# Results scattered without add and summed per batch, in a static order of blocks

## The chip, the cores and the metric

One core of a Trainium2 chip runs one layer of a small language model. The metric is the device time of one execution in microseconds (us); less is better.

## The reference

Each of 8 x 512 tokens looks up 36 angles, a circuit of six qubits turns them into six expectation values, and these are projected to an embedding of 192. An attention layer and a mixture of experts with two of eight experts per token follow, each behind a layer norm and added to its input.

```python
def reference(x, L0_tok_quantum_params, ...):
    h = _L0_tok_ref(x, L0_tok_quantum_params, L0_tok_post_w, L0_tok_post_b)
    h = h + _L0_attn_ref(_layernorm(h, axis=-1), L0_attn_W_qkv, L0_attn_b_qkv)
    h = h + _L0_ffn_ref(_layernorm(h, axis=-1), L0_ffn_Wg, L0_ffn_W1, L0_ffn_b1, L0_ffn_W2, L0_ffn_b2)
    return h

def _L0_ffn_ref(x, Wg, W1, b1, W2, b2):
    gate_scores = jnp.einsum('bsd,de->bse', x, Wg)
    topk_scores, topk_idx = jax.lax.top_k(gate_scores, K)          # K = 2, E = 8
    topk_probs = jax.nn.softmax(topk_scores, axis=-1)
    h = jax.nn.gelu(jnp.einsum('bsd,edh->bseh', x, W1) + b1, approximate=False)
    y = jnp.einsum('bseh,eho->bseo', h, W2) + b2
    y_sel = jnp.take_along_axis(y, topk_idx[..., None], axis=2)
    return jnp.sum(topk_probs[..., None] * y_sel, axis=2)
```

## The kernel before

The kernel is written out by hand, engine by engine; each engine runs its own list in order, and semaphores hold the lists together. It has three parts.

The *front* (to about 190 us) computes the circuit and, batch by batch, attention, the gate scores and the residual. In its last iterations VectorE finds the two experts of each token of a batch (`route_and_root`), the row at which the token goes into that expert's region (`slots`), and its share (`shares`). GpSimd scatters the tokens' 32 features into `routed`, a scratch tensor in device memory with a region of rows for each expert: `scatter(b, k)`, eight scatters of 128 rows for each batch, 64 in all. TensorE computes the residual of the batch (`residual`), ScalarE copies it to `hres` (`h2_copy`), and SyncE stores it to `out` (`store`).

The *table*: when all batches are routed, `counts` sums the tokens of each expert, and VectorE works out (`block_table`) for each of 71 blocks of 128 rows which expert it has (`t_exp`) and at which row of `routed` it starts (`t_i`). Blocks stand in the order of experts; there are 64 + 7 of them so that every split of the tokens fits, and the last ones can be empty. A second table says up to which block all additions must have landed before a block may be scattered, since a token's two results are added to the same row of `out`.

The *blocks*: four blocks make a step. SyncE loads a block's rows into `xb` (`load_block`, 16 blocks ahead); TensorE transposes a step (`block_transpose`), picks the step's four up projections (`pick_up`, from VectorE's `expert_of`) and applies them (`up_proj`); ScalarE applies gelu; TensorE multiplies with the expert's down projection (`down_proj`) into one of two buffers; VectorE weights the result into one of eight buffers `y` (`weighted`); GpSimd adds it to `out` by an indirect scatter with add. SyncE counts the scatters that have landed in `landed`:

```python
for m in range(BLOCKS):
    last_shared = pool.value_load(t_i[0:1, 1, m:m + 1], min_val=1, max_val=BLOCKS + 1)
    pool.wait_ge(y_done, m + 1)
    pool.wait_ge(landed, last_shared)
```

## Time and profile before

| | us |
|---|---|
| median of 3 runs (lowest, highest) | 389.87 (388.54, 391.79) |
| span of the profiled execution | 338.6 |
| median less that span | 51.3 |
| GpSimd busy in the span | 250.2 (74%) |
| TensorE matmul busy | 240.9 (71%) |
| VectorE busy | 177.6 (52%) |
| ScalarE busy | 95.2 (28%) |

The span runs from the first to the last instruction that the profiler records on the core; what the timed runs have beside it (loading, start and end) isn't in the profile. The profiled execution has no time of its own beside its span, so it is set beside the median of the runs. GpSimd's busy time on a scatter is the time of the instruction, and the transfer lands later.

### The profile page before, as it was taken

What the parts mean: (1) busy time and instruction counts of PE and PEld (TensorE: products, weight loads), DVE (VectorE), ACT (ScalarE), POOL (GpSimd) and SP (SyncE); (2) the same over time, 40 slices, a digit from 0 to 9 for tenths busy, and PEclk for the clock granted to TensorE, in tenths of its full rate; (3) what the DMA queues carried; (4) which work ended last, traced back from release to release, by engine and by line L of the source; (5) the groups of instructions that cost most, each with busy time, mean ns of one, the idle gap of its engine ahead of it and who ended that gap; (6) DMA issues with size and microseconds to landing.
All of it is one profiled execution on the core that took longest, in us unless ns stands there. A gap on an engine that the chain in (4) does not pass through costs nothing. (4 is left out here: it accounts for less than half of the span.)

```text
span 338.6 us, 6221 instructions
## 1 busy us (share of the span) xinstructions
PE 240.9 (71%) x1585; PEld 162.0 (48%) x1585; DVE 177.6 (52%) x698; ACT 95.2 (28%) x223; POOL 250.2 (74%) x283
## 2 busy tenths in 40 slices
PE   0831973668478989768654899999999587999500
PEld 0621641223243445444421678777777365877400
DVE  5758997488998866684699322232222122122200
ACT  1002001354324144634233323332432132133000
POOL 5778979309968777766777388888883888888673
PEclk9999995558955556965555599999999799699955
DMA  6710019900000001111123146656461556564510
GB/s 191 201 13 11 0 45 400 382 5 2 2 0 9 12 13 60 63 57 60 59 70 103 22 54 69 64 62 67 53 69 18 60 62 65 61 69 50 59 10 0
DMA packets 28141, 22.61 MB, mean 67 GB/s; under 512 B 15434, under 2 KB 25546, under 8 KB 27787
## 3 DMA queue, kind: packets, MB, share of 16 engines
q0 software_dynamic: 13296, 7.95, 21.1%
q1 hardware_dynamic: 14524, 14.23, 13.0%
q8 instruction: 15, 0.25, 0.3%
q14 instruction: 18, 0.15, 0.2%
q10 hardware_dynamic: 288, 0.03, 0.1%
HBM read 7.25 MB, written 15.63 MB: 68 GB/s over the span
## 5 line engine op out<-in xcount | busy, mean ns | idle before, releaser
L709 POOL DMA_INDIRECT out<-up x71 | 110.3, 1554 | 33.1 <-issue 13.9
L1972 PE MATMUL bank_b<-down,up 128*128 x426 | 91.2, 354 | 5.0 <-DVE up L1473 1.0
L1972 PEld LDWEIGHTS bank_b<-down,up 128*128 128x128 f32 x426 | 72.9, 200 | 22.6 <-issue 18.8
L1473 DVE TENSOR_SCALAR up<-bank_b,up 128x192 f32<-128x192 f32 x71 | 29.6, 418 | 97.5 <-PE bank_b L1972 84.9
L657 POOL DMA_INDIRECT routed<-rows,slot x64 | 61.9, 968 | 23.9 <-issue 18.0
L472 POOL DMA_INDIRECT theta_all<-angles,ids x32 | 32.4, 1012 | 10.9 <-issue 9.0
L1651 ACT ACTIVATE up<-bank_a 128x384 f32<-128x384 f32 x71 | 31.3, 497 | 3.4 <-PE bank_a L1962 2.9
L1775 PE MATMUL bank_b<-queries_t,keys_t 32*128 32x512 f32 x64 | 26.1, 900 | 6.9 <-ACT keys_t L1499 3.4
L1782 PE MATMUL bank_a<-keys_t,wt 32*128 32x512 f32 x64 | 27.6, 949 | 3.8 <-DVE nmax L1133 2.1
L1663 ACT COPY up<-bank_c 128x384 f32<-128x384 f32 x18 | 8.6, 478 | 61.8 <-PE bank_c L1951 58.7
L1133 DVE TENSOR_REDUCE nmax<-bank_a 128x2 f32<-128x1024 f32 x16 | 19.5, 1219 | 11.5 <-PE bank_a L1782 11.3
L1521 ACT ACTIVATE prob<-bank_b 128x1024 f32<-128x1024 f32 x16 | 16.4, 1023 | 18.2 <-PE bank_b L1775 18.2
L1951 PE MATMUL bank_c<-up_all,up 128*128 128x384 f32 x36 | 16.6, 545 | 6.6 <-DVE up L1418 4.4
L1962 PE MATMUL bank_a<-up 32*128 32x128 f32 x426 | 18.5, 304 | 0.6 <-ACT up L1657 0.5
L1962 PEld LDWEIGHTS bank_a<-up 32*128 32x128 f32 x426 | 15.1, 201 | 5.6 <-issue 4.5
L1848 PE MATMUL bank_a<-m,a2t 32*128 32x192 f32 x64 | 14.3, 536 | 4.8 <-ACT hres L1529 2.7
L1848 PEld LDWEIGHTS bank_a<-m,a2t 32*128 32x128 f32 x64 | 7.7, 277 | 11.9 <-issue 10.6
L1794 PE MATMUL bank_c<-prob,u 128*32 128x128 f32 x256 | 12.6, 361 | 0.8 <-ACT prob L1521 0.7
L1657 ACT COPY up<-bank_d 128x128 f32<-128x128 f32 x18 | 4.8, 266 | 25.3 <-PE bank_d L1944 25.3
L1775 PEld LDWEIGHTS bank_b<-queries_t,keys_t 32*128 32x128 f32 x64 | 7.1, 255 | 9.9 <-issue 8.6
L1794 PEld LDWEIGHTS bank_c<-prob,u 128*32 128x32 f32 x256 | 9.3, 145 | 5.0 <-ACT prob L1521 2.3
L1951 PEld LDWEIGHTS bank_c<-up_all,up 128*128 128x128 f32 x36 | 6.9, 212 | 8.5 <-issue 3.3
(420 smaller groups left out, 369.4 us busy)
## 6 DMA issues: line engine op xcount, KB each, us to landing
routed<-pad_rows SPq DMA_DIRECT2D x8, 528.0 KB, 5.7
out<-hres SPq DMA_DIRECT2D x8, 384.0 KB, 2.4
down<-down_w SPq DMA_DIRECT2D x1, 2304.0 KB, 11.9
up<-up_w SPq DMA_DIRECT2D x1, 1536.0 KB
out<-up POOLq DMA_INDIRECT x71, 3.5
up<-routed SPq DMA_DIRECT2D x69, 16.0 KB
routed<-rows,slot POOLq DMA_INDIRECT x64
up<-up_w SPq DMA_DIRECT2D x1, 780.0 KB
```

Source lines behind the costliest of these rows:

```text
L472: pool.indirect_dma_start(out=theta_all[:, t, :], out_offset=None, in_=angles, in_offset=bass.IndirectOffsetOnAxis(ids[:, b, j:j + 1], 0)) ...
L657: pool.indirect_dma_start(out=routed, out_offset=bass.IndirectOffsetOnAxis(slot[:, b, k, j:j + 1], 0), in_=rows[:, b, k, j, :], in_offset=None
L709: pool.indirect_dma_start(out=out_rows, out_offset=bass.IndirectOffsetOnAxis(xb[:, m // STEP % RING, m % STEP, DEST:DEST + 1].bitcast(I32) ...
L1473: dve.tensor_scalar(y[:, m % RESULTS, :], bank_b[:, m % 2, 0:D], xb[:, m // STEP % RING, m % STEP, SHARE:SHARE + 1], None, ALU.mult).then_ ...
L1651: act.activation(hid[:, n, :], bank_a[:, n, 0:HID], ACT.Gelu).then_inc(gelu_done, 1)
L1775: mm = pe.matmul(bank_b[:, n, :], keys_t[r, bt % 3, k * P:(k + 1) * P], queries_t[r, :], start=True, stop=True)
L1782: mm = pe.matmul(bank_a[:, n, :], wt[r, bs % 2, :], keys_t[r, bs % 3, :], start=True, stop=True)
L1794: mm = pe.matmul(bank_c[j * F:(j + 1) * F, 0:P], u[:, b * TILES + k, :], prob[:, k, j * P:(j + 1) * P], start=(k == 0), stop=(k == TILES - 1),
L1848: mm = pe.matmul(bank_a[:, 2 + n, 0:D], a2t[r, :], m2[r, :], start=True, stop=True)
L1951: pe.matmul(bank_c[:, 0:HID], pick[:, s % 2].rearrange("p n f -> p (n f)"), up_all[:, :], start=True, stop=True).then_inc(picked, 1)
L1962: mm = pe.matmul(bank_a[:, n, c * P:(c + 1) * P], up_now[r, s % 2, c * P:(c + 1) * P], xt[r, 0, :], start=True, stop=True)
L1972: mm = pe.matmul(bank_b[:, m % 2, 0:D], hid[:, m % STEP, c * P:(c + 1) * P], down[:, bass.ds(first + c * D, D)], start=(c == 0), stop=(c = ...
```

## The change

Results are no longer added to `out` where they land. Each token has a row for its first and one for its second expert in a new scratch tensor `results` (2 x 4096 rows of 192), and GpSimd scatters each block there without add and without a wait on other scatters. The residual stays in `hres`. SyncE loads the results of one batch at a time back into `prob` and `keys_t`, VectorE adds both to `hres` (`add_results`), and SyncE stores the batch.

So that a batch is whole before the last block, the order of the blocks is now by groups: the full blocks that the first four batches give (at least 25, so 25 of them stand in an early table that is made while batches 4 to 7 are still in the front), then what batches 3, 4, 5, 6 and 7 complete, one group each. After block `whole_after(b)` batch b has all its results. A late table with the other 46 blocks is made after the front; TensorE spreads it over the partitions (`late_columns`). The first 16 blocks are loaded as soon as the early scatters have landed, and the first two picks and the first transposition stand inside the front's loop.

The batches are summed after fixed blocks (`SUM_AT`), loaded and stored after fixed blocks (`STORE_AT`, `whole_after`); the last batch is loaded when the last block with tokens has landed, and summed and stored in two halves.

```diff
+    EARLY = 2 * EARLY_BATCHES * SEQ // P - (E - 1)
+    LATE = BLOCKS - EARLY
+    LEAST = 2 * TOKENS // P
+    results = nc.dram_tensor("results", (2 * TOKENS, D), F32, kind="Internal").ap()
+    results_view = results.rearrange("(k b p j) d -> b p k (j d)", k=2, b=BATCHES, j=TILES)
...
+        def whole_after(b):
+
+            return 2 * SEQ * (max(b + 1, EARLY_BATCHES)) // P + E - 2
...
+        SUM_AT = (46, 48, 53, 55, 59, 62)
+        STORE_AT = (45, 47, 51, 53, 57, 60)
...
+            def load_results(b):
+                sp.dma_start(results_in[b % 2], results_view[b]).then_inc(results_back[b % 2], 16)
+
+            def store(b):
+                sp.wait_ge(summed, b + 1)
+                sp.dma_start(out_view[b], hres[:, b, :]).then_inc(out_done, 16)
+
             sp.wait_ge(table_done, 1)
...
+            sp.wait_ge(scattered_early, 16 * 2 * TILES * EARLY_BATCHES)
+            for m in range(RING * STEP):
+                load_block(m)
+            for m in range(LEAST - 1):
                 sp.wait_ge(added[m % RESULTS], 16 * (m // RESULTS) + 16)
...
+                following = m + RING * STEP
+                if following == EARLY_STEPS * STEP:
+                    sp.wait_ge(table_done, 2)
+                    sp.wait_ge(scattered_late, 16 * 2 * TILES * (BATCHES - EARLY_BATCHES))
+                if following < BLOCKS:
+                    load_block(following)
+                if m == whole_after(0):
+                    load_results(0)
+                    load_results(1)
+                for b in range(BATCHES - 2):
+                    if m == STORE_AT[b]:
+                        store(b)
+                        if b < 3:
+                            load_results(b + 2)
+                for b in (5, 6):
+                    if m == whole_after(b):
+                        load_results(b)
+            last = sp.value_load(need[0:1, 0:1], min_val=1, max_val=BLOCKS - LEAST + 1)
+            sp.wait_ge(landed, last)
...
+            sp.wait_ge(summed, BATCHES - 2)
+            for h, cut in enumerate(LAST_HALVES):
+                sp.dma_start(results_in[1][:, :, cut], results_view[BATCHES - 1][:, :, cut]).then_inc(half_back[h], 16)
+            store(BATCHES - 2)
+            for h, cut in enumerate(LAST_HALVES):
+                sp.wait_ge(summed, BATCHES + h)
+                sp.dma_start(out_view[BATCHES - 1][:, cut], hres[:, BATCHES - 1, cut]).then_inc(out_done, 16)
...
-            pool.wait_ge(h2_out, 16 * BATCHES)
-            pool.wait_ge(order_done, 1)
             for m in range(BLOCKS):
-                last_shared = pool.value_load(t_i[0:1, 1, m:m + 1], min_val=1, max_val=BLOCKS + 1)
                 pool.wait_ge(y_done, m + 1)
-                pool.wait_ge(landed, last_shared)
-                hold(pool)
                 pool.indirect_dma_start(
-                    out=out_rows, out_offset=bass.IndirectOffsetOnAxis(
+                    out=results, out_offset=bass.IndirectOffsetOnAxis(
                         xb[:, m // STEP % RING, m % STEP, DEST:DEST + 1].bitcast(I32), 0),
-                    in_=y[:, m % RESULTS, :], in_offset=None, bounds_check=TOKENS - 1,
-                    oob_is_err=False, compute_op=ALU.add).then_inc(added[m % RESULTS], 16)
+                    in_=y[:, m % RESULTS, :], in_offset=None, bounds_check=2 * TOKENS - 1,
+                    oob_is_err=False).then_inc(added[m % RESULTS], 16)
...
+            early_table()
+            expert_of(0)
+            expert_of(1)
+
             for i in range(LAST[0] + 2, BATCHES + 2):
                 variance2(i - 2)
...
-            block_table()
-            expert_of(0)
-            expert_of(1)
...
+            late_table()
+            late_numbers()
+
+            def add_results(b, k):
...
+                if k == 0:
+                    dve.wait_ge(results_back[b % 2], 16 * (b // 2) + 16)
+                else:
+                    join()
+                last = dve.tensor_tensor(hres[:, b, :], hres[:, b, :], results_in[b % 2][:, k, :], ALU.add)
...
+                for b in range(BATCHES - 2):
+                    if m in (SUM_AT[b], SUM_AT[b] + 1):
+                        add_results(b, m - SUM_AT[b])
+            add_results(BATCHES - 2, 0)
+            add_results(BATCHES - 2, 1)
+            for h, cut in enumerate(LAST_HALVES):
+                part = hres[:, BATCHES - 1, cut]
+                dve.wait_ge(half_back[h], 16)
+                step(dve.tensor_tensor(part, part, results_in[1][:, 0, cut], ALU.add))
+                join()
+                dve.tensor_tensor(part, part, results_in[1][:, 1, cut], ALU.add).then_inc(summed, 1)
...
+            act.activation(gelu_ahead[:, :], half_pi[:, 0:1], ACT.Gelu)
             a2t_copy(BATCHES - 1)
             h2_copy(BATCHES - 1, 0)
             h2_copy(BATCHES - 1, 1)
-            act.activation(gelu_ahead[:, :], half_pi[:, 0:1], ACT.Gelu)
...
+            for m in range(LEAST - 1, BLOCKS):
+                act.wait_ge(added[m % RESULTS], 16 * (m // RESULTS) + 16)
+                act.sem_inc(landed, 1)
...
+                if i == BATCHES:
+                    pick_up(0)
+                    pick_up(1)
+                    block_transpose(0)
 
             residual(BATCHES - 1, 0)
             residual(BATCHES - 1, 1)
-            pe.wait_ge(table_done, 1)
-            pick_up(0)
-            pick_up(1)
             pe.wait_ge(down_in, 16)
             pe.wait_ge(h2_copied, 2 * BATCHES)
-            block_transpose(0)
             up_proj(0)
+            late_columns()
             for m in range(BLOCKS):
```

VectorE, ahead of the front's last four iterations; `nmax` is the row maximum of batch 7, `t` the copy with which batch 4 is routed. Before:

```order
L1133 TENSOR_REDUCE nmax<-bank_a 128x2 [waits s_done]
L1178 COPY t<-bank_a 128x96 [waits t2_done]
L1181 TENSOR_TENSOR var_p<-t,ev 128x64 [waits t2_copied]
L1184 TENSOR_REDUCE var_s<-var_p 128x4 [waits dve_step]
L1186 TENSOR_SCALAR ve<-var_s 128x4 [waits dve_step]
```

And now (`angle_stages` holds the table's work space, `up` the picks):

```order
L1167 TENSOR_REDUCE nmax<-bank_a 128x2 [waits s_done]
L1418 TENSOR_SCALAR full_i<-full_i 128x8
...
L1425 TENSOR_TENSOR angle_stages<-blk,cum 128x175 [waits dve_step]
L1428 TENSOR_REDUCE t_exp<-angle_stages 128x25 [waits dve_step]
L1429 TENSOR_TENSOR angle_stages<-angle_stages,skip 128x175
L1432 TENSOR_REDUCE t_skip<-angle_stages 128x25 [waits dve_step]
L1433 TENSOR_SCALAR up<-t_exp,own 128x25
L1434 TENSOR_SCALAR t_i<-t_exp 128x25
L1436 SCALAR_TENSOR_TENSOR t_i<-blk,t_skip 128x25 [waits dve_step]
L1495 TENSOR_TENSOR up<-feature,up 128x128 x2
L1214 COPY t<-bank_a 128x96 [waits t2_done]
```

The early table and two picks, 19 instructions, stand between the row maximum and the routing of batch 4.

TensorE, where the front's iteration for batch 5's residual (`bank_a<-m,a2t`) begins. Before:

```order
L1813 MATMUL bank_a<-var_w,at 128x96 [waits at_copied]
L1838 MATMUL bank_a<-ident,ev 128x128 [waits h2_copied,wt_copied,gates_done]
L1848 MATMUL bank_a<-m,a2t 128x192 [waits wt_copied,h2_copied,t2_copied,a2t_copied]
L1848 MATMUL bank_a<-m,a2t 128x192
L1848 MATMUL bank_a<-m,a2t 128x192 [waits wt_copied,h2_copied,t2_copied,a2t_copied]
```

And now:

```order
L1887 MATMUL bank_a<-var_w,at 128x96 [waits at_copied]
L1918 MATMUL bank_a<-ident,ev 128x128 [waits h2_copied,wt_copied,gates_done]
L1946 MATMUL bank_b<-up_all,up 128x384 [waits exp_done,pick_done] x2
L1935 MATMUL bank_d<-ident,up 128x128 [waits block_in0]
L1928 MATMUL bank_a<-m,a2t 128x192 [waits wt_copied,h2_copied,t2_copied,a2t_copied]
```

The two picks and the first transposition of a block step moved here from behind the last residual.

VectorE at the end of the program, `up<-bank_b` being the weighting of a block. Before nothing stands behind the last one; now:

```order
L1538 TENSOR_SCALAR up<-bank_b,up 128x192 [waits added6,y_mm]
L1528 TENSOR_TENSOR hres<-hres,prob 128x768 [waits results_back0]
L1528 TENSOR_TENSOR hres<-hres,prob 128x768 [waits dve_step]
L1553 TENSOR_TENSOR hres<-hres,keys_t 128x384 [waits half_back0]
L1555 TENSOR_TENSOR hres<-hres,keys_t 128x384 [waits dve_step]
L1553 TENSOR_TENSOR hres<-hres,keys_t 128x384 [waits half_back1]
L1555 TENSOR_TENSOR hres<-hres,keys_t 128x384 [waits dve_step]
```

Batch 6 is added whole and batch 7 in halves, after the weighting of all 71 blocks.

## Rows read from the trace of the kernel before

**Rows 1.** The page's granted clock, in tenths of full speed, 40 slices of 8.5 us

```profile
PEclk9999995558955556965555599999999799699955
```

**Rows 2.** Groups by line: count, busy us and mean ns, idle before and its releasers

```profile
L709 POOL DMA_INDIRECT out<-up x71 | 110.3, 1554 | 33.1 <-issue 13.9 <-SPq L446 9.7 <-DVE up L1473 9.4
...
L657 POOL DMA_INDIRECT routed<-rows,slot x64 | 61.9, 968 | 23.9 <-issue 18.0 <-DVE ev L1162 5.6 <-DVE slot L1269 0.3
```

**Rows 3.** Timeline of GpSimd: start us, us, instruction, idle before and releaser

```profile
189.19 0.96 POOL L657 DMA_INDIRECT routed<-rows,slot  x1 [0.31 <-issue]
...
252.54 1.55 POOL L709 DMA_INDIRECT out<-up  x1 [0.30 <-issue]
256.87 1.55 POOL L709 DMA_INDIRECT out<-up  x1 [2.77 <-issue]
...
322.71 1.55 POOL L709 DMA_INDIRECT out<-up  x1 [2.83 <-issue]
...
332.01 1.56 POOL L709 DMA_INDIRECT out<-up  x1 [0.30 <-issue]
```

**Rows 4.** Timeline of VectorE in the block stage: blocks 5, 37, 41, 65 and 70

```profile
201.56 0.42 DVE L1473 TENSOR_SCALAR up<-bank_b,up 128x192 f32<-128x192 f32 x1 [0.84 <-PE bank_b L1972]
...
253.77 0.42 DVE L1473 TENSOR_SCALAR up<-bank_b,up 128x192 f32<-128x192 f32 x1 [0.98 <-PE bank_b L1972]
...
264.36 0.42 DVE L1473 TENSOR_SCALAR up<-bank_b,up 128x192 f32<-128x192 f32 x1 [4.13 <-DMA out<-up]
...
311.13 0.42 DVE L1473 TENSOR_SCALAR up<-bank_b,up 128x192 f32<-128x192 f32 x1 [0.87 <-PE bank_b L1972]
...
318.26 0.42 DVE L1473 TENSOR_SCALAR up<-bank_b,up 128x192 f32<-128x192 f32 x1 [0.72 <-PE bank_b L1972]
```

**Rows 5.** Timeline of VectorE, GpSimd and TensorE where batch 4 is routed

```profile
140.93 0.25 DVE L1178 COPY t<-bank_a 128x96 f32<-128x96 f32 x1
...
148.52 0.95 POOL L657 DMA_INDIRECT routed<-rows,slot  x1 [1.86 <-DVE ev L1162]
...
149.18 1.09 PE L1755 MATMUL bank_d<-ident,w_rep 128*128 128x128 f32 x4 [2.21 <-issue]
```

**Rows 6.** Timeline of VectorE in the table: first, a reduction, last, a product

```profile
175.23 0.17 DVE L1375 TENSOR_SCALAR count_i<-bank_a 128x16 int32<-128x16 f32 x1
...
178.22 1.05 DVE L1398 TENSOR_REDUCE t_exp<-angle_stages 128x71 f32<-128x497 f32 x1
...
181.79 0.17 DVE L1412 TENSOR_SCALAR need<-steps_late 128x4 int32<-128x4 f32 x1
...
184.78 0.67 DVE L1459 TENSOR_TENSOR angle_stages<-angle_stages,shared_last 128x497 f32<-128x497 f32 x1
```

**Rows 7.** Timeline of TensorE and ScalarE from batch 5's residual to the first block

```profile
168.97 1.01 PE L1848 MATMUL bank_a<-m,a2t 32*128 32x192 f32 x4 [1.39 <-issue]
...
180.35 0.48 ACT L1529 COPY hres<-bank_a 128x384 f32<-128x384 f32 x1 [1.19 <-PE bank_a L1848]
180.85 1.28 ACT L1668 ACT_TABLE_LOAD   x1
...
186.06 1.62 PE L1951 MATMUL bank_c<-up_all,up 128*128 128x384 f32 x2 [2.15 <-ACT up L1663]
...
188.42 1.67 PE L1962 MATMUL bank_a<-up 32*128 32x128 f32 x24 [0.52 <-ACT up L1657]
```

**Rows 8.** Stretches: length, busy us by engine, clock, DMA share, GB/s

```profile
50.00:59.00 9.00, 2.41 (x9) 1.43 (x9) 7.04 (x18) 1.18 (x3) 7.89 (x7) 0.59 1.01 399
...
200.00:210.00 10.00, 9.64 (x89) 7.76 (x88) 2.90 (x8) 3.34 (x9) 8.17 (x7) 1.00 0.58 65
...
324.00:326.00 2.00, 0.00 (x0) 0.00 (x0) 0.00 (x0) 0.00 (x0) 1.70 (x2) 0.50 0.41 41
```

**Rows 9.** DMA issues of the page: count, KB each, median us to landing

```profile
out<-hres SPq DMA_DIRECT2D x8, 384.0 KB, 2.4
...
out<-up POOLq DMA_INDIRECT x71, 3.5
```

More of the change, by code:

```diff
@@ L431, in _ @@
-            sp.sem_inc(landed, 1)
-            sp.wait_ge(table_done, 1)
-            first_rows = [block_row(m) for m in range(0, STEP, 2)]
-            sp.wait_ge(scattered, 16 * (2 * TILES * SEEN - 1))
-            rows_written(0)
-            sp.sem_inc(first_ready, 1)
-            for m, row in zip(range(0, STEP, 2), first_rows):
-                load_block(m, row)
-            for r in range(1, RING):
-                rows_written(r)
-                for m in blocks_of(r):
-                    load_block(m, block_row(m))
@@ L451, in _ @@
+            sp.wait_ge(out_done, 16 * (BATCHES + 1))
         @block.gpsimd
@@ new lines, in down_proj @@
+            def down_proj(m):
+                first = pe.value_load(t_i[0:1, 1, m:m + 1], min_val=0, max_val=(E - 1) * HC * D)
+                if m < 2:
+                    pe.wait_ge(up_now_copied, m + 1)
+                pe.wait_ge(gelu_done, m + 1)
+                if m >= 2:
+                    pe.wait_ge(y_done, m - 1)
+                for c in range(HC):
+                    mm = pe.matmul(bank_b[:, m % 2, 0:D], hid[:, m % STEP, c * P:(c + 1) * P], down[:, bass.ds(first + c * D, D)],
+                                   start=(c == 0), stop=(c == HC - 1))
+                mm.then_inc(y_mm, 1)
@@ L1858, in _, with late_columns @@
+            def late_columns():
+                pe.wait_ge(late_ready, 1)
+                pe.matmul(bank_c[:, 0:2 * LATE], ones[:, :], late_diag[:, :, :].rearrange("p a m -> p (a m)"),
+                          start=True, stop=True).then_inc(late_spread, 1)
             pe.wait_ge(weights_done, 3)
```

362 lines of the change are left out of this document (183 added, 179 removed).

## Prediction

> **What bounds the kernel now.** Start with the page's slices of the granted clock [rows 1]: the slices from 152 to 195 us lie at half of full speed (1.2 instead of 2.4 GHz), and from 195 us to the last block it is full except in a few slices around 265 and 290 us. So the program has a thin front up to about 190 us and a dense block stage behind it. The groups by line [rows 2] name who works there: GpSimd issues 71 result scatters of 1554 ns, and the 64 scatters that route the tokens take 968 ns each. The timeline of GpSimd [rows 3] then shows the stage: the result scatters follow each other with 0.30 us between them, so 1.86 us a block, and two places are worse: 2.77 us before block 32 and 2.83 us before block 65, where the scatter waits until earlier additions to the same rows have landed. The last scatter starts at 332.01.
>
> VectorE's timeline [rows 4] has the rate of the others. Its one short instruction per block is released by TensorE, and between block 5 (201.56) and block 37 (253.77) it shows 52.21 us for 32 blocks: **1.63 us a block**. GpSimd needs 1.86, so it falls behind, the eight result buffers fill up, and block 41 waits 4.13 us for a scatter to land (264.36). TensorE goes idle there and gets half the clock afterwards. The last block is weighted at 318.26, 14 us before GpSimd starts its last scatter. **GpSimd bounds the block stage, TensorE is next at 1.63 us, and TensorE loses time only through GpSimd.**
>
> **Routing scatters.** These also run on GpSimd, back to back, and their last one starts at 189.19 [rows 3]; no result scatter can start before 190.15. One more thing to see is how many blocks carry tokens. After block 65's scatter at 322.71 the DMA moves 41 GB/s (324 to 326 us, [rows 8]); the five scatters behind it move next to nothing, since their rows are all out of range. So 66 blocks are real and the last five are empty.
>
> **The change, part by part.** The profiled span is 338.6 us, the median of the timed runs 389.87, so 51.3 us lie around the span; I leave these as they are and move the span alone.
>
> *Early table, on VectorE.* It now stands between the row maximum of batch 7 and the t copy of batch 4, where VectorE goes on without a pause at 140.93, and where TensorE waits for it: its next transposition at 149.18 stood idle for 2.21 us, and GpSimd's scatters of batch 4, at 148.52, for 1.86 us [rows 5]. So this work is on the path. The old table ran from 175.23 to 181.96 [rows 6], 6.73 us, with four wide instructions (two reductions of 1.05, two products of about 0.67: 3.4 us). They shrink from 497 to 175 elements, to about 1.2 us, and some six of the small ones go, 0.9 us: 6.7 - 2.2 - 0.9 = 3.6, with the two expert picks at 0.25 each 4.1 us. Bounds: 1.9 (if the 2.21 us that TensorE was idle can be given back some other way) and 4.5. I take **4.1**, since no engine ahead of that place has slack.
>
> *Picks moved ahead on TensorE.* Two products like the one at 186.06 (1.62 us at half clock) and a transposition with a third of the columns: 3.7 us, now in front of the residual of batch 5 at 168.97, which had 1.39 us of idle time before it [rows 7]. Between 1.0 and 2.3 us of it shows; I take **2.0**. ScalarE's three copies for them fit in its gaps. ScalarE's table load (1.28 us, 180.85) now stands ahead of the last a2t copy instead of behind the last residual: 0 to 1.3, I take **0.9**.
>
> *Start of the blocks.* The residual's last copy ended at 180.83, and the first up projection started at 188.42 [rows 7], because table, picks and transposition stood between them. Now nothing but the copy itself does: 180.83 + 4.1 + 2.0 + 0.9 = 187.8. Of the 7.6 us taken out, 7.0 are paid in front: **-0.6 us**. The late table (some 35 small instructions at about 0.15 us, 5 us from about 181.3) is ready for the late columns, which TensorE reaches at 189.5; what is queued behind that wait is every block, and its cover is 3 us thick. The late columns fit in the time in which TensorE waits for the first gelu.
>
> *Scatters without add.* The nearest rows: 968 ns for a scatter of 32 values a row without add, 1554 ns for 192 values with it [rows 2]. The row is either as long because of the add or because of the bytes; both ends stay in the range. I take 0.97 to 1.0, because both handle 128 rows and the add is the one difference in kind. With 0.30 us between, 1.27 to 1.3 us a block is less than TensorE's 1.63. The Trainium skill, Perfetto Trace Analysis, section DMA Instruction — SWDGE (GPSIMD), says that such a row ends when the last descriptor is written, not when the data has moved; by that rule the bytes don't count, the sum stands as here, and no row of this trace alone proves it. GpSimd starts 4.1 us later than before (194.3), one or two blocks behind, and catches up 0.35 us a block, within the eight buffers. The waits on landed additions are gone with it.
>
> *Block stage.* At TensorE's rate block 65 is weighted at 201.56 + 60 x 1.632 - 0.6 = 298.9 instead of 311.13, and the five empty blocks take 7.13 us as before (318.26 - 311.13, [rows 4]): block 70 at 306.0, ends 306.4. That is **-12.3 us**, the start included. The twelve additions among the blocks (128x768) cost, from 0.67 us for 497 elements [rows 6], an estimate of 1.0 us each. VectorE's gaps are 0.9 to 1.7 us in each block and TensorE may run one block ahead, so I cost them at nothing; without that cover each would cost up to 0.2 us, 2.4 in all. That row also ran beside a routing scatter (one started at 184.15) and neither was stretched. The Trainium skill, SBUF — State Buffer, section Who interferes with whom, says that a VectorE instruction with two inputs in SBUF contends with a GpSimd instruction that reads SBUF, and the later one waits; what it would make of the sum is a rival below.
>
> *Loads and stores of results.* SyncE issues the loads of batches 0 and 1 (786 KB each) after block 38's scatter has landed: weighted at 254.8, landed about 259. VectorE wants batch 0 after block 46 (267.9) and batch 1 after block 48 (271.1). The bulk transfers at 50 to 59 us moved 399 GB/s with the DMA engines full [rows 8], so two loads take 4 us and their latency: some 3 to 5 us to spare. Costed at nothing. A load that is late stops VectorE, behind it the freeing of TensorE's output, and with it every block.
>
> *Tail.* Before, 19.9 us lay between the end of the last weighting (318.68) and 338.6. Now VectorE adds batch 6 (two of 1.0) and batch 7 in halves (four of 0.55): 306.4 + 4.2 = 310.6. Batch 7's load waits for block 65 only (weighted 298.9, landed about 303), so both halves are in by 308 under the five empty blocks: free. A store of 384 KB lands in 2.4 us [rows 9]; with batch 6's just ahead I take 3.4 (2.4 to 4.8): 314.0. Before, the last scatter started at 332.01 and landed some 3.5 us later [rows 9], 3.1 us before the end; I keep these 3.1: 317.1. **-21.5 us**: 389.87 - 21.5 = **368.4 us**.
>
> **The rivals.**
> - *The scatter is long by its bytes.* For it: the 968 ns rows carry 128 bytes, the 1554 ns rows 768. Then GpSimd still bounds: 194.6 + 65 x 1.86 = 315.5 for block 65's scatter, landed 319, loads until 323.5, the last half added 324.6, stored 327, end 330.1: -8.5, so 381.4 us.
> - *Loads late, or additions held up.* The DMA engines were 58% busy with the adding scatters at 65 GB/s [rows 8]. The new traffic is 9.4 MB of loads and stores within some 50 us. If scatters and loads hold each other up so that VectorE waits twice or three times for 2 us, and TensorE's clock drops once for it, the cost is 5 to 10 us: 373 to 379. By the SBUF page's rule each addition would wait for, or hold up, a scatter of 0.97 us: 12 times at most 1 us over the gap, 12 us, 380; a mechanism of this kernel, but the row at 184.78 speaks against it.
> - *The front costs less.* If the early table falls into a wait, blocks start 3 to 5 us earlier: 363 to 365. Against: VectorE had no gap from 140.93 to the idle row of TensorE.
> - *The transfers can't be carried: slower.* From block 38 on, 6.3 MB of loads, 3.1 MB of stores and 2.7 MB of scatters have to move in about 44 us, 275 GB/s. If they went at the rate of the adding scatters (65 GB/s at 0.58, so 112 GB/s when full) they would take 108 us, to 367, and the run 423 us. It decides at 186 GB/s (65 us), below which the kernel is slower than before. The 399 GB/s of [rows 8] speaks against it.
> - *It doesn't do what it says.* If the order of the late blocks leaves SyncE waiting so that blocks come late, the gain of the stage is lost: about 390.
>
> **How the numbers follow.** First forecast 0.60 (364 to 373); late loads or held-up additions 0.14; scatter by bytes 0.12; cheap front 0.08; transfers 0.04; nothing gained 0.02. The predicted time is the likeliest's, 368.5. From 362 to 381.5 leaves out the last two and half of the byte case, about 0.12, and some of the edges. The three runs spread by 3 us, so 1% is about what can be told from no change. Faster by over 1%: 0.93; within 1%: 0.03; slower: 0.04.
>
> **What would show it.** Result scatters of about 1.0 us, 0.3 apart at first, then released by VectorE; no wait of over 1 us in VectorE's weighting after block 5 and a full clock in every slice from 200 us to the last block; first up projection at 186 to 189 although table and picks are gone from there; last weighting at about 306; end some 11 us behind it. Wrong if scatters stay at 1.55, if an addition waits for its load, or if the routing scatters end later than 196.

## The result, and the profile after

| | us |
|---|---|
| kernel before, median of 4 runs (lowest, highest) | 390.03 (388.54, 391.79) |
| changed kernel, median of 4 runs (lowest, highest) | 371.89 (366.24, 377.56) |
| ratio of the times (95% interval) | 0.944 (0.938 to 0.951) |
| span of the profiled execution, and its own time | 364.5, 366.24 |
| GpSimd busy | 211.8 (58%) |
| TensorE matmul busy | 237.6 (65%) |
| VectorE busy | 185.9 (51%) |

The ratio is made without the runs that the comparison counts as disturbed, so it stands for the lower of the times. Forecast were 368.5 us and a ratio of 0.945. The first thing to see is that the span (364.5) is only 1.7 us shorter than its execution's own time. Where the prediction set a span of 338.6 beside 390 us, it had the profile of an execution that was some 50 us shorter than those that are timed. So before and after can't be compared by these two profiles; the first experiment gives the one that was missing.

The page of the changed kernel, first the granted clock in slices of 9.1 us (against [rows 1]), then the groups by line (against [rows 2]):

```profile
PEclk9999975597565556566555655899999999999995
...
L740 POOL DMA_INDIRECT results<-up x71 | 71.4, 1006 | 64.5 <-DVE up L1538 46.0
...
L691 POOL DMA_INDIRECT routed<-rows,slot x64 | 62.2, 972 | 52.8 <-DVE ev L1196 35.5
```

A result scatter takes 1006 ns instead of 1554. GpSimd no longer bounds the block stage: 46.0 us of its idle time ahead of the scatters now end with VectorE's result. Ahead of the routing scatters it waits 35.5 us for VectorE, which it did for 5.6 us in [rows 2]. The front has become slower also where nothing was added to it.

Timeline of GpSimd (start us, us, instruction, idle before and releaser), against [rows 3]:

```profile
218.91 0.96 POOL L691 DMA_INDIRECT routed<-rows,slot  x1 [0.31 <-issue]
229.31 1.00 POOL L740 DMA_INDIRECT results<-up  x1 [9.44 <-DVE up L1538]
...
354.81 0.99 POOL L740 DMA_INDIRECT results<-up  x1 [0.30 <-issue]
```

The last routing scatter starts at 218.91 instead of 189.19. Timeline of VectorE: early table, end of the picks, then blocks 5, 37, 41, 65 and 70, against [rows 4, 5, 6]:

```profile
153.85 0.16 DVE L1418 TENSOR_SCALAR full_i<-full_i 128x8 int32<-128x8 int32 x1
...
157.58 0.25 DVE L1214 COPY t<-bank_a 128x96 f32<-128x96 f32 x1
...
236.74 0.42 DVE L1538 TENSOR_SCALAR up<-bank_b,up 128x192 f32<-128x192 f32 x1 [0.85 <-PE bank_b L1969]
...
294.17 0.42 DVE L1538 TENSOR_SCALAR up<-bank_b,up 128x192 f32<-128x192 f32 x1 [1.00 <-issue]
...
301.31 0.42 DVE L1538 TENSOR_SCALAR up<-bank_b,up 128x192 f32<-128x192 f32 x1 [0.89 <-issue]
...
345.26 0.42 DVE L1538 TENSOR_SCALAR up<-bank_b,up 128x192 f32<-128x192 f32 x1 [0.89 <-PE bank_b L1969]
...
352.37 0.42 DVE L1538 TENSOR_SCALAR up<-bank_b,up 128x192 f32<-128x192 f32 x1 [0.70 <-PE bank_b L1969]
```

The early table with its picks takes 3.73 us (153.85 to 157.58). Block 41 no longer waits 4.13 us. But from block 5 to 37 there are 57.43 us, 1.79 a block, where [rows 4] had 1.63.

Timelines of ScalarE and TensorE at the start of the blocks, against [rows 7], with one of the long waits ahead of it:

```profile
176.87 0.27 ACT L1601 COPY context_t<-bank_c 128x128 f32<-128x128 f32 x1 [9.29 <-remote]
...
222.74 0.48 ACT L1605 COPY hres<-bank_a 128x384 f32<-128x384 f32 x1 [2.36 <-PE bank_a L1928]
```

```profile
223.31 1.67 PE L1957 MATMUL bank_a<-up 32*128 32x128 f32 x24 [1.78 <-issue]
```

As said, nothing but the residual's last copy stands between front and blocks (223.22 to 223.31, where [rows 7] had 7.6 us). But it all comes at 223 and not at 188, since ScalarE has stood still for 9.29, 8.50 and 7.49 us. The input of the copy at 176.87 was the work of matmuls whose rows end at 168.8; "remote" says that no row explains the release. Such waits, in which an engine stands still though its input seems ready, are called *stops* below.

### The profile page after: what moved, and what is told of

It reads as the page before. It is cut to its first block, busy times and chain, and to the rows that moved or that the text cites. A ratio compares the mean times of both kernels' runs of the same rounds, so it can differ in the third digit from the quotient of the medians.

```text
span 364.5 us, 5901 instructions
## 1 busy us (share of the span) xinstructions
PE 237.6 (65%) x1586; PEld 162.0 (44%) x1586; DVE 185.9 (51%) x724; ACT 95.3 (26%) x223; POOL 211.8 (58%) x285
## 4 chain that ended last, share of the span: by engine, by line
PE 39%; issue 20%; POOL 15%; DVE 10%; another core or an unknown queue 6%; ACT 5%; DMA 2%; ACTq 0%; POOLq 0%; SPq 0%
PE bank_b L1969 17%; PE bank_a L1957 4%; PE bank_c L1946 4%; PE bank_a L1856 3%; PE bank_b L1849 3%; DVE nmax L1167 2%; PE bank_a L1928 2%; POOL theta_all L508 2%; POOL rs L680 2%; ACT up L1635 2%; POOL results L740 1%; DMA results<-up 1%; POOL routed L691 1%; DMA keys_t<-results 1%
## 5 line engine op out<-in xcount | busy, mean ns | idle before, releaser
L740 POOL DMA_INDIRECT results<-up x71 | 71.4, 1006 | 64.5 <-DVE up L1538 46.0
L1969 PE MATMUL bank_b<-down,up 128*128 x426 | 88.2, 345 | 13.9 <-ACT up L1635 11.6
L691 POOL DMA_INDIRECT routed<-rows,slot x64 | 62.2, 972 | 52.8 <-DVE ev L1196 35.5
L1969 PEld LDWEIGHTS bank_b<-down,up 128*128 128x128 f32 x426 | 70.1, 193 | 31.6 <-issue 27.9
L1856 PE MATMUL bank_a<-keys_t,wt 32*128 32x512 f32 x64 | 29.0, 994 | 5.4 <-DVE nmax L1167 4.1
L1167 DVE TENSOR_REDUCE nmax<-bank_a 128x2 f32<-128x1024 f32 x16 | 19.5, 1219 | 16.2 <-PE bank_a L1856 16.2
L1957 PE MATMUL bank_a<-up 32*128 32x128 f32 x426 | 18.1, 298 | 1.8 <-issue 1.8
L1868 PE MATMUL bank_c<-prob,u 128*32 128x128 f32 x256 | 14.8, 384 | 3.9 <-DVE slot_e L1204 2.1
L1868 PEld LDWEIGHTS bank_c<-prob,u 128*32 128x32 f32 x256 | 10.6, 153 | 8.7 <-issue 6.5
L1605 ACT COPY hres<-bank_a 128x384 f32<-128x384 f32 x16 | 7.6, 478 | 25.3 <-PE bank_a L1928 13.0
L1946 PE MATMUL bank_c<-up_all,up 128*128 128x384 f32 x32 | 12.9, 486 | 0.0
L1819 PE MATMUL bank_a<-ident,w 128*128 128x128 f32 x8 | 3.5, 439 | 11.4 <-DVE w L1162 9.1
L1856 PEld LDWEIGHTS bank_a<-keys_t,wt 32*128 32x128 f32 x64 | 7.3, 276 | 8.1 <-issue 7.0
```

The costliest lines, as they stand in the source:

```text
L691: pool.indirect_dma_start(out=routed, out_offset=bass.IndirectOffsetOnAxis(slot[:, b, k, j:j + 1], 0), in_=rows[:, b, k, j, :], in_offset=None
L740: pool.indirect_dma_start(out=results, out_offset=bass.IndirectOffsetOnAxis(xb[:, m // STEP % RING, m % STEP, DEST:DEST + 1].bitcast(I32), 0),
L1167: dve.tensor_reduce(nmax[:, b % 2, 2 * h:2 * h + 2], bank_a[:, 0:2, :], AX.X, ALU.max, negate=True).then_inc(max_done, 1)
L1856: mm = pe.matmul(bank_a[:, n, :], wt[r, bs % 2, :], keys_t[r, bs % 3, :], start=True, stop=True)
L1946: pe.matmul(picked_in(s), pick[:, s % 2].rearrange("p n f -> p (n f)"), up_all[:, :], start=True, stop=True).then_inc(picked, 1)
L1957: mm = pe.matmul(bank_a[:, n, c * P:(c + 1) * P], up_now[r, s % 2, c * P:(c + 1) * P], xt[r, 0, :], start=True, stop=True)
```

## The experiments

A profile of one kernel can fall on one of its longer or shorter executions: they spread by 2 to 11 us within one comparison, and the median of the unchanged kernel before was 381, 386, 381 and 389 us in the four comparisons below. Times are therefore given beside the kernel before of the same comparison, and terms are read between the same two places of two traces.

**The kernel before once more.** No edit.

> The kernel before, unchanged, to have a profile of an execution of the usual length. The only profile so far has a span of 338.6 us beside a median of 390 us, while the changed kernel's span is 1.7 us short of its own time. First theory: some 50 us of the usual executions lie inside the span, as stretches in which engines stand still while nothing that the profile shows holds them; then the span is about 388 us and such stretches are seen, in the front too. Rival: the profiled execution is like the others and 51 us lie around the span; then the span is 339 us beside 390. The time is 390 us in both.

Measured: 378.33 us beside 380.70; the span is 377.6 us of an execution of 379.38. The first theory holds: the time lies inside the span. ScalarE's timeline, first this kernel, then the 338.6 us profile at the like place:

```profile
176.21 0.27 ACT L1525 COPY context_t<-bank_c 128x128 f32<-128x128 f32 x1 [5.95 <-remote]
...
191.40 0.27 ACT L1525 COPY context_t<-bank_c 128x128 f32<-128x128 f32 x1 [6.98 <-remote]
```

```profile
162.14 0.27 ACT L1525 COPY context_t<-bank_c 128x128 f32<-128x128 f32 x1 [1.90 <-PE bank_c L1794]
```

So the stops belong to the kernel before as well, in its usual executions. One more thing follows: this kernel is the kernel before, and yet its ratio to it is 0.989 (0.982 to 0.995). About 1.2% is what a mere repetition can show.

**The changed kernel once more.** No edit.

> The changed kernel, unchanged. In its profile ScalarE stood still for 9.3 and 8.5 us before two context_t copies and 7.5 us before an hres copy, with its input long computed. First theory: these stops come with SyncE's burst of block loads beside GpSimd's scatters, so they stand at the same places in every execution. Rival: they fall anywhere (instruction fetch or the like), so their places and their sum differ. 366 to 378 us by both.

Measured: 361.19 us beside 380.70, both lower than the first times, with the ratio 0.948 (0.943 to 0.954); the profile is of an execution of 368.06 (span 366.3). The long waits of ScalarE ahead of context copies are again there, at 182.74 (9.13 us) and 196.40 (6.93), and ahead of hres at 226.92 (7.22). Their places are those of the program, not those of the clock: that part of the expectation holds. (A further one, of 6.60 us, stands at 147.94, where the first profile has none.) Like with like, in us of each span:

| | before, again | changed | changed, again |
|---|---|---|---|
| first up projection | 226.68 | 223.31 | 227.50 |
| block 5 weighted | 240.54 | 236.74 | 240.89 |
| block 65 weighted | 350.03 | 345.26 | 346.12 |
| block 70 weighted | 357.30 | 352.37 | 353.93 |
| last scatter starts | 371.10 | 354.81 | 356.37 |
| span | 377.6 | 364.5 | 366.3 |

**Twelve of the first sixteen loads later.**

```diff
             for m in range(RING * STEP):
+                if m == STEP:
+                    sp.wait_ge(scattered_late, 16 * 2 * TILES * (BATCHES - EARLY_BATCHES))
                 load_block(m)
```

> SyncE loads only the first four blocks behind the early scatters and the other 12 behind the last routing scatter. If the stops of ScalarE, TensorE and SyncE from 167 to 177 and from 184 to 192 us come from the early burst of loads beside the scatters, both go and the first up projection comes at about 205 instead of 223 us: 350 to 356 us in all. If they don't depend on the loads, the time stays within 3 us of the changed kernel's or is 1 to 3 us longer, since block 4's rows come later.

Measured: 370.28 us beside 380.70, ratio 0.966 (0.956 to 0.976). The stops stay as they were (8.95 us before the context copy at 183.12, 6.96 before that at 196.81), and the first up projection comes at 227.91. SyncE's burst has no part in them; the theory falls. The time is 9 us above the 361.19 of the changed kernel in the same comparison, where 1 to 3 us at most were expected: later loads cost something of their own. Between the two profiles it is 3.7 us (spans 370.0 and 366.3), 1.5 of them by block 5; the rest is not explained.

**The kernel before without the add.**

```diff
                     in_=y[:, m % RESULTS, :], in_offset=None, bounds_check=TOKENS - 1,
-                    oob_is_err=False, compute_op=ALU.add).then_inc(added[m % RESULTS], 16)
+                    oob_is_err=False).then_inc(added[m % RESULTS], 16)
```

> The kernel before with its result scatters writing instead of adding, waits and order kept, so that out holds one of the two results alone: the operation of the scatter by itself. If the 1.55 us come from the add, the row is 1.0 us at the same 192 values, GpSimd is no longer the bound, and the last block's scatter starts some 14 us earlier: 374 to 379 us. If they come from the bytes, the row stays 1.55 us and the time 390 us; the changed kernel's 1.0 us would then need another cause (the tensor it writes to).

Measured: 372.06 us beside 380.70, ratio 0.979 (0.974 to 0.985), so 8.6 of the change's 19.5 us (374 to 379 us were expected). `out` then holds only one of a token's two results. Its group in the page:

```profile
L709 POOL DMA_INDIRECT out<-up x71 | 70.1, 987 | 71.4 <-DVE up L1473 32.3
```

The same 192 values, 987 ns: the row was long by the add, not by the bytes. The gain lies at the end: from the start of the last weighting to the end of the span there are 11.5 us instead of 20.3. Blocks 5 to 65 take 110.3 us, no less than the 109.5 of the kernel before, and blocks 9 to 33 take 1.82 us each here too (248.52 to 292.11). The slower pace is no matter of the new tensor or the new order, it comes with the short scatter. The other 10.9 us of the change belong to the new order, the tables and the sum together; no run separates them. Timelines of one step, all engines in one, show where: of the kernel before once more, then of the changed one once more.

```profile
262.25 0.81 PE L1951 MATMUL bank_c<-up_all,up 128*128 128x384 f32 x2
...
263.09 0.48 ACT L1663 COPY up<-bank_c 128x384 f32<-128x384 f32 x1 [3.09 <-PE bank_c L1951]
```

```profile
263.84 0.81 PE L1946 MATMUL bank_c<-up_all,up 128*128 128x384 f32 x2
...
265.41 0.74 DVE L1538 TENSOR_SCALAR up<-bank_b,up 128x192 f32<-128x192 f32 x2 [2.87 <-PE bank_b L1969]
265.45 0.48 ACT L1647 COPY up<-bank_c 128x384 f32<-128x384 f32 x1 [3.73 <-PE bank_c L1946]
...
266.46 0.42 PE L1969 MATMUL bank_b<-down,up 128*128 x1 [0.83 <-ACT up L1635]
```

The picks take 0.81 us in both, but ScalarE copies them 0.84 us after their start in one and 1.61 us in the other, and VectorE weights two blocks back to back at 265.41, as if it had heard of both at once. ScalarE's gelu is then late and TensorE idle for 0.83 us: once a step, 0.65 us or so of 7.17. It looks like the small form of the stops in the front: **TensorE's work is done by its rows, and the engines that wait for it are released late.**

The semaphore records in the traces say which half is late. Before the copy at 176.87 of the changed kernel, the increments of three of TensorE's products, whose rows end at 168.83, 169.60 and 170.46, are dated 176.85, 176.91 and 176.97, and ScalarE starts 0.02 us behind the first. In the step above the picks' increment comes 0.01 us behind the end of their row (263.07) in the kernel before once more, and 0.78 us behind it (265.43) in the changed one. So the increment is late, and the waiting engine answers it at once. The ends of TensorE's rows are modelled, so by these alone the product itself might be late; VectorE's rows below show the same without TensorE.

**GpSimd padded.**

```diff
+        filler = sb("filler", [P, 512])
...
                     oob_is_err=False).then_inc(added[m % RESULTS], 16)
+                step(pool.memset(filler[:, :], 0.0))
+                join()
```

`join` waits for GpSimd's own earlier memset.

> The changed kernel with a memset of 512 values on GpSimd behind each result scatter, so that GpSimd is as busy per block as before (some 1.8 us). In the changed kernel a block takes 1.79 us (weighted 9 to 33) and 1.63 us in the kernel before, and once a step ScalarE's copy of the picks starts 1.2 to 1.4 us behind the pick instead of 0.52. First theory: this comes from the phase in which short scatters and the picks meet; with the padding the copy is back at 0.52 us and the pace from block 9 to 25 at 1.63 to 1.65 us. Rival: it comes from the missing add or the new tensor and not from the phase; then the copy stays at 1.3 us and the pace at 1.79. The total is 0 to 8 us longer than the changed kernel's by both, since GpSimd then bounds.

Measured: 406.92 us beside 385.85, ratio 1.056 (1.046 to 1.065); longer than either expected, since the memset with its join makes the distance of two scatters 2.30 us and not 1.8:

```profile
240.31 0.99 POOL L741 DMA_INDIRECT results<-up  x1 [0.78 <-POOL filler L746]
241.28 0.56 POOL L746 MEMSET filler<- 128x512 f32 x1
242.61 0.99 POOL L741 DMA_INDIRECT results<-up  x1 [0.78 <-POOL filler L746]
```

What it was made for is seen: as long as the eight buffers aren't full, blocks 5 to 17 take 19.46 us, 1.62 each, and the copy stands 0.84 or 0.85 us behind the start of the picks in 13 of 16 steps (in the changed kernel in one, in the kernel before once more in 14 of 18). TensorE can go at its old pace with scatters without add. The windows of the three kernels say the same (length, busy us of TensorE matmul, weight load, VectorE, ScalarE, GpSimd, clock, DMA share, GB/s): changed, before once more, padded.

```profile
240.00:280.00 40.00, 35.19 (x284) 28.16 (x287) 10.31 (x29) 13.71 (x36) 21.89 (x23) 1.00 0.21 62
```

```profile
240.00:280.00 40.00, 38.76 (x318) 31.08 (x320) 11.42 (x31) 14.20 (x38) 33.59 (x22) 1.00 0.59 65
```

```profile
240.00:256.00 16.00, 15.68 (x119) 12.63 (x118) 4.63 (x12) 5.85 (x15) 10.68 (x14) 1.00 0.19 51
```

TensorE is busy for 88%, 97% and 98%, at full clock each time.

**Loads by the step.** SyncE waits for a step's four scatters and then issues four loads.

```diff
...
-                if following < BLOCKS:
-                    load_block(following)
+                if m % STEP == STEP - 1:
+                    for n in range(following - STEP + 1, min(following + 1, BLOCKS)):
+                        load_block(n)
```

> SyncE issues the four block loads of a step together, behind the landing of its fourth block, instead of one behind each landing. If the late copy of the picks (1.2 to 1.4 us behind the pick) comes from SyncE's waits and loads between the picks, the pace from block 9 to 33 goes from 1.79 towards 1.63 us and the time falls by 3 to 8 us. If SyncE has no part in it, pace and time stay (within 1%).

Measured: 367.96 us beside 385.85, ratio 0.957 (0.949 to 0.966); pace 1.81 us from block 9 to 33. SyncE has no part in it.

**The early table twice.**

```diff
...
+            early_table(False)
             early_table()
```

> The early table computed twice in a row on VectorE, the second time for use. By the prediction it costs 3.6 us and stands on the path: the first up projection comes 3 to 4 us later and the time rises by 3 to 4 us. Rival: the front now has a slack that hides it (the wait of VectorE of 3.5 to 12 us for the context of the next batch); then the time stays within 1 us.

Measured: 371.02 us beside 385.85, ratio 0.964 (0.956 to 0.971), 3.1 us over the kernel above, of the same comparison. VectorE's timelines, that kernel's and this one's, where batch 4 is routed:

```profile
158.29 0.25 DVE L1215 COPY t<-bank_a 128x96 f32<-128x96 f32 x1
```

```profile
161.99 0.25 DVE L1214 COPY t<-bank_a 128x96 f32<-128x96 f32 x1
```

3.70 us there and 4.42 at the first up projection (223.82 and 228.24). The table is on the path and costs what it takes.

**No loads of results, no additions.** Both `load_results` and the additions go, and the stores write the residual.

```diff
...
-                last = dve.tensor_tensor(hres[:, b, :], hres[:, b, :], results_in[b % 2][:, k, :], ALU.add)
...
+                if k == 1:
+                    dve.sem_inc(summed, 1)
```

> The changed kernel without the loads of results and without the additions; the stores write the residual alone, so the experts' part is missing in the output. By the prediction the loads and the additions among the blocks cost nothing and only the tail shrinks, by the 4.2 us of additions behind the last weighting and the wait for the last load: 4 to 6 us less, the pace from block 41 to 65 unchanged. Rival (loads and additions hold blocks up): the stretch from block 41 to 65 gets 3 us or more shorter as well, 8 to 12 us less in all.

Measured: 367.27 us beside 385.85, ratio 0.959 (0.948 to 0.969); no different from the 367.96 of the kernel with everything (the one with loads by the step). Blocks 41 to 65 take 43.71 us against 43.95 in the changed kernel's first profile. So 6.3 MB of loads and the additions among the blocks are free, as forecast; but so is the tail, which wasn't. The last rows of both show why: GpSimd of this kernel, then SyncE's store and GpSimd of the changed one.

```profile
354.33 0.99 POOL L730 DMA_INDIRECT results<-up  x1 [0.30 <-issue]
```

```profile
356.32 1.39 SPq L484 DMA_DIRECT2D out<-hres  x2
```

The last scatter starts at 354.33 here and the span ends at 364.0, 9.7 us later. In the changed kernel it starts at 354.81 and the span ends at 364.5: 9.7 us too, although its last stores have landed 5 us before (SyncE's wait for them is over at 359.24). What comes last is GpSimd's closing drain; the trace has it from 353.34 to 364.3 us. In the kernel before once more 6.5 us lay between the last scatter (371.10) and the end, without the add 8.4.

**The last batch in one piece.**

```diff
-        LAST_HALVES = (slice(0, TILES * D // 2), slice(TILES * D // 2, TILES * D))
+        LAST_HALVES = (slice(0, TILES * D),)
...
```

> The last batch loaded, summed and stored in one piece instead of two halves. By the prediction the halves are loaded free under the empty blocks, and only the last store is shorter for them: one piece ends 1 to 1.5 us later. Rival: a store of half the size lands no sooner, so nothing changes (within 0.5 us behind the last weighting, 12.2 to 12.3 us now).

Measured: 363.47 us beside 381.00, ratio 0.950 (0.944 to 0.956); 12.15 us from the last weighting to the end, as with halves (12.1 and 12.4). The halves buy nothing, since the drain ends last.

**A small distance behind each result scatter, and behind each routing scatter.** The filler has 128 values; the second kernel has the same two lines behind the scatter to `routed`.

```diff
                     oob_is_err=False).then_inc(added[m % RESULTS], 16)
+                join()
+                step(pool.memset(filler[:, :], 0.0))
```

> The changed kernel with a memset of only 128 values on GpSimd behind each result scatter, so that two scatters start 1.5 to 1.6 us apart at least instead of 1.3, still below TensorE's 1.63 us. Theory: TensorE's signals are held up while scatters without add follow each other at 1.3 us; a little more room ends it, the copy of the picks stands 0.52 us behind the pick, the pace from block 9 to 33 is 1.63 to 1.66 us and the time falls by 4 to 9 us against the changed kernel (366 us there beside 386 before). Rival: 1.5 us is not enough room (or the distance has no part in it): pace 1.79 us and the same time within 1%.

> The same memset behind each of the 64 routing scatters only (1.26 us apart so far, eight in a row for each batch). Theory: the stops of 5 to 9 us in which TensorE's results reach ScalarE late lie over the rows of eight scatters and end with them; with 1.5 us between starts they go, the eight take 12 us instead of 10, and the first up projection comes at 200 to 212 us instead of 223 to 227. Rival: the stops have another cause or the room is too small; then they stay, each as long as its eight scatters, and the first up projection comes 3 to 15 us later than now.

Measured: 368.31 us (361.96 to 372.41) beside 381.00, ratio 0.951, and 365.17 us (359.56 to 367.95), ratio 0.950. The memset of 0.22 us fills most of the 0.30 us that was there anyway, so starts stand 1.35 to 1.37 us apart, not 1.5. The pace is 1.80 us behind padded result scatters. Behind padded routing scatters there are stops of 9.15 and 5.59 us; the first up projection came at 218.46, earlier than in either profile of the changed kernel, but a further stop of 9.60 us behind it put block 5 at 239.09, where it was. Nothing is told apart by this pair but that 1.37 us is not enough.

**A wide distance behind both.** 512 values behind a routing scatter, 384 behind a result scatter.

> The small memsets moved the starts of two scatters only from 1.27 to 1.35 us apart, and nothing changed. Here the memset has 512 values behind a routing scatter (about 1.7 us from start to start) and 384 behind a result scatter (about 1.6 us, just below TensorE's 1.63). Theory: it is the distance of scatters without add that decides, at some value between 1.37 us (held up) and 2.3 us (not held up); if it lies below 1.6, the copy of the picks is 0.52 us behind the pick, the pace from block 9 to 33 is 1.63 to 1.67 us, and the stops in the front go. Rival: the value is higher, or it is not the distance but GpSimd's waiting for blocks in between that counts; then the pace stays at 1.75 to 1.79 us, the front gets 5 to 20 us longer since eight scatters take 13.6 us, and the time is 370 to 390 us.

Measured: **343.71 us (340.56 to 348.24) beside 389.19 (383.71 to 392.46)**, about 12% less than the kernel before and less than every execution of the changed one (360.64 to 377.56, in other comparisons; its medians there are 17 and 28 us above), by 135 memsets that compute nothing. Page, TensorE, VectorE and GpSimd:

```profile
PEclk9999996567855555895557579799999999999995
```

```profile
180.28 0.96 POOL L692 DMA_INDIRECT routed<-rows,slot  x1 [0.17 <-issue]
181.95 0.96 POOL L692 DMA_INDIRECT routed<-rows,slot  x1 [0.17 <-issue]
...
212.14 0.96 POOL L692 DMA_INDIRECT routed<-rows,slot  x1 [0.17 <-issue]
213.81 1.00 POOL L743 DMA_INDIRECT results<-up  x1 [0.17 <-issue]
215.40 1.00 POOL L743 DMA_INDIRECT results<-up  x1 [0.17 <-issue]
```

```profile
193.26 1.67 PE L1962 MATMUL bank_a<-up 32*128 32x128 f32 x24 [0.62 <-issue]
```

At 1.67 us from start to start no wait in the front is "remote" any more, and the first up projection comes at 193.26, 30 us before that of the changed kernel and near the forecast 187.8.

All of the gain is in the front. From block 5 to 65 this kernel takes 112.1 us, where the changed one took 108.5 and 105.2. At first GpSimd holds it up: its routing ends at 213, and blocks 8 to 12 wait for a result buffer (5.62 us before block 8). Then it does so no longer. From block 9 to 33 its scatters stand 1.59 us apart, and the weightings are 1.79 us apart and released by TensorE. In four of the 16 steps the increments are late again, the copy of the picks 1.56 to 2.32 us behind their start:

```profile
262.88 0.81 PE L1951 MATMUL bank_c<-up_all,up 128*128 128x384 f32 x2
...
264.40 0.74 DVE L1543 TENSOR_SCALAR up<-bank_b,up 128x192 f32<-128x192 f32 x2 [2.88 <-PE bank_b L1974]
264.44 0.48 ACT L1652 COPY up<-bank_c 128x384 f32<-128x384 f32 x1 [3.69 <-PE bank_c L1951]
```

So 1.67 us is enough in the front and 1.58 to 1.59 us is not among the blocks, where 2.30 us and the adding scatters' 1.86 us were. Result scatters 1.7 to 1.8 us apart, and the routing padding alone, remain to be tried.

VectorE's late table shows the late increments without TensorE. In the changed kernel a wait of VectorE for its own last instruction lasts 1.85 us while GpSimd's eight scatters run: that instruction ended at 212.41, its increment is dated 214.24. In this kernel, beside scatters 1.67 us apart, the same copy has no wait, though it took 0.67 us and not 0.17:

```profile
214.27 0.17 DVE L1409 COPY run_end<-run_end 128x16 f32<-128x16 f32 x1 [1.85 <-remote]
```

```profile
190.59 0.67 DVE L1414 COPY run_end<-run_end 128x16 f32<-128x16 f32 x1
```

## Why the prediction held, and where it did not

The time and the ratio came out as forecast (368.5 against 371.89 us, 0.945 against 0.944), but not by all of its steps. Several of its own signs failed. The first up projection was to come at 186 to 189 us and the last weighting at about 306; they came at 223.3 and 352.4. Routing scatters that end later than 196 us were to prove it wrong; they end at 219.9. In the kernel before once more the last of them starts at 218.55 and the last weighting at 357.30, so for these the base was off, not the change. And weightings were to wait for no more than 1 us after block 5; the next one waited 2.52.

- *"51.3 us lie around the span"*: wrong. 1.7 us do. The profile before was of an execution without the stops. The forecast survived because the stops stand in both kernels, which it did not know: first up projection at 226.68 before, 223.31 and 227.50 after.
- *Early table* 4.1 us: 3.73 measured in place, 3.70 when done twice. *Start of the blocks* -0.6 us: -3.4 and +0.8 between like executions. The two stand on either side of the forecast, so the trade (7.6 us taken out, about as much paid in front) fits, but the length of the stops hides it. The late table took 20 us (205.8 to 226.3) instead of 5, since its waits were among those held up; it ended behind the first up projection and held up no block.
- *Scatters without add* 0.97 to 1.0 us: 1.006, and 0.987 in the kernel before. The rule of the Trainium skill, Perfetto Trace Analysis, section DMA Instruction — SWDGE (GPSIMD), that the row ends with the last descriptor, agrees: six times the bytes of a routing scatter cost 34 ns.
- *Block stage*: **this step failed in its size.** "At TensorE's rate" of 1.632 us the 60 blocks from 5 to 65 were to take 97.9 us; they took 108.5 and 105.2, against 109.5 in the kernel before once more. The 11.7 us forecast for them (12.3 with the start) became 1 to 4. The waits for GpSimd went as forecast, but 0.16 us a block came in their place. 1.62 us a block is TensorE's pace where scatters stand 2.3 us apart; beside scatters that follow at 1.3 us its increments came late once a step.
- *Loads, stores and additions at nothing*: right, by the kernel without them. Where the first two loads ran (300 to 310 us) 224 GB/s flowed at a DMA share of 0.69, so 325 GB/s when full, an estimate between the 112 and the 399 GB/s that [rows 8] gave. An addition took 950 ns (1.0 forecast), and none was stretched; the scatters beside them were, four of 71, at most from 0.98 to 1.77 us at 335.25. By the Trainium skill, SBUF — State Buffer, section Who interferes with whom, the later of the two waits; the trace agrees, and since GpSimd had time the rival's price was 0.
- *Tail* of 11.1 us from the start of the last weighting: 12.1 to 12.4, against 20.3 before, so 7.9 to 8.2 us less where 9.2 were forecast. The size is near, the reason wrong: not additions (4.2) and a store (3.4) end the kernel but GpSimd's drain, 9.7 us behind the last scatter. The gain is that GpSimd starts its last scatter 2.4 us behind the last weighting, not 13.8.

These terms sum to -11 to -13 us between profiled executions, while the timed medians differ by 18.1 and 19.5. In the second comparison the changed kernel's profile fell on its longest execution, 368.06 beside a median of 361.19. The kernel with the last batch in one piece has a profile at its median (363.31 us), and beside the kernel before once more its span is 16.0 us shorter: 5.4 us up to block 5, 2.9 from there to block 65, 8.1 in the tail, less 0.5 in the empty blocks. So with the block stage at a quarter of its forecast, the total came out partly by luck: in that profile the front, with its stops, was some 5 us shorter than in the kernel before, which no step had foreseen. Of the rivals, the two about traffic are out (no sum: no gain), and so is the scatter by its bytes.

## What to carry to other kernels

Look at the profiled execution's own time before its span is used as a base; if they differ by more than a few us, profile the unchanged kernel again. When an engine is made faster, ask what its new rhythm does to engines that share nothing with it in the program: here 0.55 us less per scatter cost 0.16 us per block on TensorE, and 0.4 us of idle work ahead of the next routing scatter took 30 us out of the front. And what is last in a kernel is found by leaving work out: a whole summation behind the last block was free beside a drain.

## What the runs showed of the hardware

- Indirect scatters without add, eight or more at 1.26 to 1.37 us from start to start, go with stops of 4 to 15 us in which semaphore increments of TensorE and VectorE come late (15.10 us at 154.58 in the kernel with small padding behind result scatters). In the kernel before without the add, one of 4 us among the blocks followed five scatters. At 1.67 us there were none in the front; among the blocks late increments stayed at 1.58 us and were gone at 2.30 us and with the 1.86 us of adding scatters. In one such stretch (167 to 177 us of the changed kernel) five of SyncE's register instructions took 690 to 720 ns each, and none around it over 301.
- Why is open. The 338.6 us execution of the kernel before had the same routing scatters at 1.26 us and no stop, so the distance alone is not the cause. That execution differs in one more way: its trace holds 5707 semaphore records, and that of the same program run once more 3793. Records are missing from the traces of all other executions too, 3391 are left in that of the kernel with wide distances, so their loss alone doesn't bring stops. The Trainium skill, NOTIFIC — the notification-queue block, section 7.1 Overflow, describes that the path on which engines write their records can stall the engine that writes; no run here shows whether that happened, and the kernel with 135 memsets more to record is the one without stops in the front.
- The end of the program waits for GpSimd's drain: 6.5 to 6.6 us from the start of the last adding scatter, 8.4 us without add into `out`, 9.7 to 9.9 us into `results` (10.1 to 10.4 with padding behind result scatters).
- The same kernel, timed as another, differed by 1.2% (0.5 to 1.8).
